# A float32-accurate cross-attention block on one core: who makes the upper half of the probabilities in the first 32 items, and where parts and totals stand in a slot

## What is computed

```
q  = ln(queries) ; kv = ln(tokens)
qp, kp, vp = q @ Wq.T + bq, kv @ Wk.T + bk, kv @ Wv.T + bv
scores = qh @ kh.T / sqrt(hd) - scale[h] * dist(query, token) + offset[h]
attn = softmax(scores)                       # 16 x 16 tiles of 256 x 256
x = queries + (attn @ vh) @ Wo.T + bo
h = gelu(ln(x) @ W1.T + b1)
out = x + h @ W2.T + b2
```

## Time and profile before

| | |
|---|---|
| median of 3 runs | 1252.64 us (1251.54 to 1253.87) |
| profiled execution, its own time | 1252.53 us |
| its span, first to last instruction | 1250.7 us |
| TensorE busy | 1208.7 us, 97% |
| GpSimd, VectorE, ScalarE busy | 995.3, 978.2, 849.6 us |
| granted TensorE clock, mean | 0.992 |

### The profile page before, as it was taken

One profiled execution on the slowest core, in us unless ns is written; L12 is line 12 of the kernel. 1 busy time (PEld: TensorE's weight loads), 2 busy tenths in 40 slices (PEclk: granted clock), 3 DMA queues, 4 the chain that ended last, 5 costly groups with the idle time before them and its releaser, 6 DMA issues.

```text
span 1250.7 us, 27639 instructions
## 1 busy us (share of the span) xinstructions
PE 1208.7 (97%) x9383; PEld 814.1 (65%) x9383; DVE 978.2 (78%) x2654; ACT 849.6 (68%) x1902; POOL 995.3 (80%) x1285
## 2 busy tenths in 40 slices
PE   5888889999999999999999999999999999999998
PEld 5655456666667666666667676666666666666665
DVE  5699998888878788888878788888888787768311
ACT  5768758676777677676777677776767677766331
POOL 5478888989898898989898998989898997768320
PEclk9889999999999999999999999999999999999999
DMA  6689999888989898989899898989989897878534
GB/s 197 179 186 218 217 204 216 187 200 204 210 193 217 185 215 201 190 197 198 206 202 221 177 219 191 203 199 198 203 206 208 184 213 179 168 175 174 151 108 128
DMA packets 468588, 241.66 MB, mean 193 GB/s; under 512 B 383952, under 2 KB 408800, under 8 KB 468448
## 3 DMA queue, kind: packets, MB, share of 16 engines
q1 hardware_dynamic: 468448, 239.91, 84.7%
HBM read 109.66 MB, written 12.58 MB: 98 GB/s over the span
## 4 chain that ended last, share of the span: by engine, by line
PE 85%; DVE 8%; issue 2%; SPq 1%; ACT 1%; DMA 1%; POOL 1%; POOLq 0%; DVEq 0%; ACTq 0%
PE ps_down L621 26%; PE ps_up L606 26%; PE ps_qk L542 12%; PE ps_vo L566 6%; PE ps_vo L563 5%; PE ps_s L577 4%; PE ps_pv L591 4%; DVE p_nat L1022 2%; DVE soft L1005 1%; DVE w L950 1%; SPq L362 1%; PE ps_down L498 1%; DVE stats L968 1%; DVE x_nat L982 0%; DVE qk_parts L996 0%
## 5 line engine op out<-in xcount | busy, mean ns | idle before, releaser
L606 PE MATMUL ps_up<-hT,w 128*128 128x256 f16 x3072 | 377.2, 273 | 3.0 <-ACT u L762 1.5
L1200 POOL TENSOR_SCALAR p_nat<-soft,row_inv 128x256 f16<-128x256 f32 x512 | 329.9, 654 | 59.1 <-DVE row_inv L1016 58.0
L621 PE MATMUL ps_down<-w,hid 128*128 128x512 f16 x1536 | 372.9, 379 | 0.4 <-DVE hid L1054 0.4
L606 PEld LDWEIGHTS ps_up<-hT,w 128*128 128x128 f16 x3072 | 300.2, 98 | 93.1 <-issue 3.2
L1005 DVE CUSTOM_DVE_ANT_0 soft<-ps_s,soft,factor 128x256 f32<-128x256 f32 x512 | 225.6, 476 | 132.7 <-PE ps_s L577 132.0
L730 ACT ACTIVATE soft<-soft,neg_max 128x256 f32<-128x256 f32 x512 | 255.2, 500 | 108.4 <-DVE neg_max L1005 107.0
L1022 DVE SCALAR_TENSOR_TENSOR p_nat<-soft,row_inv,p_nat 128x256 f16<-128x256 f32 x512 | 291.5, 608 | 1.0 <-POOL p_nat L1200 0.8
L1208 POOL TENSOR_SCALAR soft<-dist,scale_neg,offset 128x512 f32<-128x512 f32 x256 | 248.5, 971 | 12.8 <-DVE p_nat L1022 12.6
L621 PEld LDWEIGHTS ps_down<-w,hid 128*128 128x128 f16 x1536 | 148.7, 97 | 131.9 <-DVE hid L1054 0.9
L762 ACT ACTIVATE u<-ps_up,bias,up_scale 128x256 f32<-128x256 f32 x256 | 142.3, 556 | 131.7 <-PE ps_up L606 130.7
L1216 POOL TENSOR_SCALAR hid<-u,hid_scale 128x1024 f16<-128x1024 f32 x64 | 80.9, 1264 | 104.4 <-ACT u L768 101.2
(11 more groups left out here) (114 smaller groups left out, 1539.1 us busy)
## 6 DMA issues: line engine op xcount, KB each, us to landing
w<-x_scratch SPq DMA_DIRECT2D x256, 256.0 KB, 3.1
stack<-qk_parts SPq DMA_DIRECT2D x256, 96.0 KB
raw<-in_ctx SPq DMA_DIRECT2D x32, 256.0 KB, 3.7
raw<-in_x SPq DMA_DIRECT2D x32, 256.0 KB, 3.1
c_stage<-in_w SPq DMA_DIRECT2D x32, 256.0 KB, 4.0
x<-in_x SPq DMA_DIRECT2D x32, 256.0 KB, 3.4
out<-x SPq DMA_DIRECT2D x32, 256.0 KB, 3.2
tok_rows<-in_tok_xy SPq DMA_DIRECT2D x16, 256.0 KB, 4.5
```

What stands on the lines that cost most here:

```text
L606: mm = e.matmul(ps_up[s % 2][:, 0:L], w_1_sb[:, wp, k, m * P:(m + 1) * P], hT[:, b % 2, :, xp * KT + k, :], start=(k, wp, xp) == (0, 0, 0) ...
L621: mm = e.matmul(ps_down[tt][:], hid[:, chunk % HID_RING, i, hp, tt * P:(tt + 1) * P], w_2_sb[:, s % W2_RING, wp, :], start=(m == 0 and (hp ...
L1200: mine = e.tensor_scalar(p_nat[:, nat, HI, lc, :], soft[:, ring, lc, :], row_inv[:, ring, lc:lc + 1], 1.0, ALU.mult, ALU.mult)
```

## The change

For the first 32 items (FIRST = 32) the split of the probabilities is made by other engines. GpSimd's `p_normalise` multiplies `soft` by `row_one` and by 2^14 in place, in float32; ScalarE's new `p_hi_first` copies it to float16, once for both row halves; VectorE's `p_lo` is one subtraction of 128x512 in place of two operations of 128x256, and `row_inv` isn't made. In slots 1 to 30 `qk_hi` comes behind `exps` on ScalarE, and on VectorE `qk_lo`, the first items' `p_lo` and `attn_lo` come at the end of the slot (`attn_lo` mostly a slot later). On TensorE the totals of W1's and W2's norms stand right behind `scores`; their `square_norm` moves from the slot after to the end of the slot of the sums. `keep_busy` begins in slot 0 and writes to `ps_pv` before slot 9. All behind item 31 is as before, apart from semaphore counts.

```
-                if 7 <= slot < DOWN:
+                if 0 <= slot < DOWN:
...
+                    taken += {0: 8, 2: 16, 4: 16}.get(slot, 0)
+                    keep_busy(ps_pv if slot < 9 else ps_down[0], max(0, SLOT_STEPS - taken))
...
+            def p_hi_first(i):
+                nat, ring = i % NAT_RING, i % SOFT_RING
+                gate.wait_ge(s_pnorm, i + 1)
+                if i >= NAT_RING:
+                    gate.wait_ge(s_pt[(i - NAT_RING) % PT_RING], n_pt(i - NAT_RING))
+                e.activation(p_nat[:, nat, HI, :, :], soft[:, ring, :, :], ACT.Copy).then_inc(s_phi_first)
...
+                for i in due(slot, 3, ITEM, FIRST):
+                    p_hi_first(i)
                 for i in due(slot, 0, ITEM, N_ITEMS):
                     exps(i)
...
+                gate.wait_ge(s_pnorm, min(2 * k - SOFT_RING + 2, FIRST))
+                gate.wait_ge(s_inv, k - FIRST // 2 - SOFT_RING // 2 + 1)
                 e.reciprocal(row_one[:, pair_of, :], row_sum[:, pair_of, :]).then_inc(s_one)
+                if k < FIRST // 2:
+                    return
...
+                if i < FIRST:
+                    gate.wait_ge(s_phi_first, i + 1)
+                    e.tensor_tensor(p_nat[:, nat, LO, :, :], soft[:, ring, :, :], p_nat[:, nat, HI, :, :], ALU.subtract).then_inc(s_plo)
+                    return
...
+                if 1 <= slot < UP:
+                    for which in range(2):
+                        for G in due(slot, QK_PROJ + 2 * which + 1, GROUP, N_HG):
+                            qk_lo(G, which)
+                for i in due(slot, 3, ITEM, FIRST):
+                    p_lo(i)
+                for G in range((UP - 11) // GROUP + 1):
+                    if slot == GROUP * G + (10 if G % HG == HG - 1 else 11):
                         attn_lo(G)
+                for w in range(AT_W1, N_W):
+                    if slot == NORM[w] - 1:
+                        square_norm(w)
...
+            def p_normalise(i):
+                ring = i % SOFT_RING
+                gate.wait_ge(s_one, i // 2 + 1)
+                for lc in range(LC):
+                    mine = e.tensor_scalar(soft[:, ring, lc, :], soft[:, ring, lc, :], row_one[:, ring, lc:lc + 1], P_SCALE, ALU.mult, ALU.mult)
+                mine.then_inc(s_pnorm)
```

More of the change, by code:

```diff
@@ L176, in build_block @@
         N_CHUNKS = MT // CH
+        FIRST = 32
         UP = 31
@@ L649, in tensor_program @@
                             next(qk)
-                for w in range(N_W):
+                for w in range(AT_W1):
                     if slot == TOTAL[w]:
@@ L772, in scalar_program @@
                     columns_square()
-                for which in range(2):
-                    for G in due(slot, QK_PROJ + 2 * which + 1, GROUP, N_HG):
-                        qk_hi(G, which)
+                if slot < 1 or slot >= UP:
+                    for which in range(2):
+                        for G in due(slot, QK_PROJ + 2 * which + 1, GROUP, N_HG):
+                            qk_hi(G, which)
                 for G in due(slot, 10, GROUP, N_HG):
@@ L1067, in vector_program @@
                     score_max(i)
+                for n in due(slot, 1, KT, 2 * N_CHUNKS):
+                    weight_sums(AT_W1 + n)
                 for k in due(slot, 2, 2, N_ITEMS // 2):
@@ L1253, in gpsimd_program @@
                     bias_tile(i)
-                for i in due(slot, 2, ITEM, N_ITEMS):
-                    p_hi(i)
+                for i in due(slot, 2, ITEM, FIRST):
+                    p_normalise(i)
+                for i in due(slot, 2 + FIRST, ITEM, N_ITEMS - FIRST):
+                    p_hi(FIRST + i)
                 for w in range(AT_W1, N_W):
```

40 lines of the change are left out of this document (22 added, 18 removed).

## The result

| | before | changed |
|---|---|---|
| median of 9 runs | 1252.06 us (1250.86 to 1253.87) | 1255.70 us (1254.78 to 1256.66) |
| profiled execution, its span | 1252.53 us, 1250.7 us | 1256.07 us, 1254.2 us |

The ratio is 1.0026, with a 95% interval of 1.0017 to 1.0035. The forecast was 1247.6 us and the range ended at 1254.

A forecast was written before the change was run, and what follows sets the result against it. VectorE was taken to bound slots 7 to 26, SyncE's queue slots 27 to 34, with a fixed length from slot 37. Terms -0.8 - 3.6 - 0.8 + 0.2 = -5.0 us gave 1247.6 us, range 1242.5 to 1254.

The forecast's parts named there:

- SyncE's queue: Slots 27 to 34: DMAs issued one after another, a fixed length hung on the moment of `w2_lo(7)`.
- ScalarE's term: Slots 7 to 26: ScalarE binds next and loses part of its waits; half the room taken, -3.6 us.
- VectorE per item: Slots 7 to 26: one subtraction at 0.84 us replaces 1.26 us, saving 0.42 per item, 8.4 us over 20 slots.
- ScalarE's own work: Slots 7 to 26: 20 copies at 0.591 us add 11.8 us to 64.09, making 75.9 us.
- The floor: Slots 7 to 26 can't get shorter than ScalarE's 75.9 us of work.
- the room of 7.3 us: Slots 7 to 26: old length 83.16 us minus ScalarE's 75.9, reached only if ScalarE loses all its waits.
- Rival A: ScalarE is the bound and keeps its waits: no change, about 1250.8 us; chance 0.17.
- GpSimd's own work: Per item, `p_normalise` costs `p_hi`'s 0.655 us, so 0 more.
- Slots 0 to 6: Only two more `p_lo`, in slots 5 and 6, count: -0.8 us; the fill counted as 0.
- Totals, norms: Slots 7 to 26: same number of operations and no wait to remove, 0 us.
- Slot 27: `p_lo` at the slot's end lets `w2_lo(7)` start earlier: -0.8 us for SyncE's queue.
- Rival B: GpSimd holds ScalarE up through `p_hi_first`'s wait for `p_normalise`: slower, stretch 87.9, time 1255.9 us; chance 0.13.

The follow-up runs named there:

- the split alone: Kernel before with only ScalarE's copies, GpSimd's normalising and the single subtraction, all at the old places in the slot: 1252.51 us, ratio 1.0005.
- GpSimd's link: Taken out by swapping two lines of the changed kernel, so that GpSimd normalises an item before making the next bias tile: 1254.68 us, ratio 1.0015.

## Why the prediction was wrong

The four corners of the late places, as ratios to the kernel before:

| | none late | key/query late | subtraction late | both |
|---|---|---|---|---|
| kernel before | 1 | 1.0008 | 1.0016 | 1.0043 |
| with the rest of the change | 0.9999 | 0.9998 | 0.9981, 0.9992 | 1.0026 |

In the lower row either move is free, and both cost about 0.3%. In the upper row either seems to cost a little, and both together more than the sum. I had looked at them one by one: late key/query parts as a gain for ScalarE, the late subtraction as a gain for SyncE's queue.

**The step that failed** is ScalarE's term, -3.6 us for slots 7 to 26, which came out at +4.8. It said that ScalarE's wait ahead of `qk_hi` "shrinks since `qk_hi` now follows the exponentials", and took that as room won. It did shrink, from 7.6 to 0.0, but it was handed to VectorE, whose lower parts wait for the upper ones, and behind VectorE's wait I had let the change put the subtraction at no cost. What the sum lacks is the next question: where a wait goes, which engine is late next, and what is queued behind it? Leaving ScalarE's part early removes the wait and the loss (1251.70); leaving the subtraction in front removes what is queued behind it, and the loss (1252.09).

**VectorE per item** was right and even too careful: the subtraction took 0.701 us, I took 0.84; busy time fell by 9.9 us where 8.4 were counted. By the rule of the Trainium skill's page "SBUF — State Buffer", section "Who interferes with whom", a subtraction that meets an idle GpSimd should take its fastest time. This trace agrees: of the 21 subtractions that fall into slots 7 to 26, the 8 beside an idle GpSimd took 0.68 us each (0.676 was the fastest in the earlier trace rows). But of the 13 that overlapped with a GpSimd operation 12 took 0.67 to 0.69 us as well, and one 1.10; beside them it was GpSimd's operations that were long, bias tiles up to 1.79 us for 0.76 alone. So the choice between 0.676 and 0.998 did not hang on whether GpSimd was idle, as I had said. The right size for the operation was of no use for the time.

**ScalarE's own work** was right: a copy took 0.619 us (0.591 taken), the stretch had 73.90 us of it (75.9 forecast). The floor was never near: the best split kernels need 81.7 to 82.3 us, since VectorE, at 72 to 74 us busy, is idle for 8 to 10 us in each of them, mostly for ScalarE's copy or the values' parts. So of the room of 7.3 us none of these kernels won more than 1.4. Rival A's view of the split (no change) is what the split alone showed: 1.0005.

**GpSimd's own work:** 0.632 us for the new form, 0.655 taken; right.

**Slots 0 to 6:** -0.8 forecast, -0.5 measured. The fill did not hold the clock: its mean was 0.80 of full speed, 0.86 before and 0.86 with totals, norms and fill alone.

**Totals, norms:** 0 forecast, 0.9997 alone, right as a sum. But slots 27 to 36 went down by 1.6 us, not 0.6, and the norms alone do that (45.93 for 47.78 us); 1.4 us come back behind slot 37, where that kernel needs 1045.50 us (204.30 to the end) in place of 1044.14.

**Slot 27:** `h_turn` came 4.23 us after the slot's start (167.38 in the trace), 4.68 before: -0.45 for -0.8.

**Rival B** hit the numbers, 1255.9 and a stretch of 87.9 for 1255.7 and 87.98, with the wrong weights. Its waits were real: 5.6 us of ScalarE for the normalised item (12 were assumed), 13.0 us of GpSimd for the subtraction, and the chain of the stretch lay on GpSimd more than on any other engine. ScalarE's other idle time, 8.1 us for the maxima, was not in B. Without GpSimd's link more than half of the loss stays (1254.68), and with ScalarE's key/query parts early all of it goes, though GpSimd's order is the same (1251.70). So B names a part of the loop; that its total was right is chance. The range ended at 1254, below B's own price, though B had a chance of 0.13.

**Open.** The late places alone on the kernel before cost more (1.0043) than inside the whole change (1.0026); these kernels also had stretches of lower clock (0.87 and, with the subtraction alone late, 0.82; 0.88 in the changed kernel and 0.94 before), in which ScalarE waited up to 8.2 us for key/query products. Whether the low clock follows from the uneven slots or adds by itself was not separated, nor how much of the changed kernel's loss runs over GpSimd. Nor was it found out why an early slot 37 gives back about 1 us behind it.

## What to carry to other kernels

When two engines work through a slot in turns, look at what stands at the end of one's slot and at the start of the other's: a consumer at the end of its slot, of something made at the end of the producer's, pushes the two towards working in turns (1279 us in the extreme case), while the same consumer ahead of every such wait costs nothing (1252.09 and 1252.31). Moving a late wait off one engine is no saving until you have said which engine has it now and what is queued behind it. And two moves that are each free need to be tried together: here both at once cost 0.3%.

## What the runs showed that I had not expected

ScalarE's copy, moved from the start to the end of its slot, cost 22 us on top of the changed kernel, though in slots 7 to 26 VectorE's and ScalarE's busy times rose by only 0.8 and 0.5 us; I had thought the two ends of a slot interchangeable. And the fill matmuls in slots 0, 3 and 6 did not raise the granted clock of that stretch (0.80 against 0.86).
